# Layer 3's rows normalised in turned form, with one PSUM bank for turns, in a four-layer graph-attention kernel

## The chip, the cores and the metric

The kernel runs on one core of a Trainium2 chip. The metric is the device time of one execution in microseconds, the median of several runs. Engines are named TensorE (PE), VectorE (DVE), ScalarE (ACT), GpSimd (POOL) and SyncE (SP).

## The reference

Eight graphs (B = 8) share one adjacency of 2048 nodes, with 64 features each. Four attention layers follow one another, and each reads a layer-normed, rectified copy of x and adds its result to x:

```
def _layernorm(x, axis=-1, eps=1e-05):
    m = jnp.mean(x, axis=axis, keepdims=True)
    v = jnp.var(x, axis=axis, keepdims=True)
    return (x - m) / jnp.sqrt(v + eps)
...
h = jnp.maximum(_layernorm(x, axis=-1), 0.0)
x = x + _L2_gnn_ref(h, adj, L2_gnn_weight, L2_gnn_query, L2_gnn_key_p)
h = jnp.maximum(_layernorm(x, axis=-1), 0.0)
x = x + _L3_gnn_ref(h, adj, L3_gnn_W, L3_gnn_a)
```

The case is about the place where the third layer's attention (layer 2 in the code, scores q·k with a leaky slope of 0.01) ends and the rows of the last layer (layer 3) are made from its result: x + attention, normalised over the 64 features, rectified, and multiplied by `L3_gnn_W`.

## The kernel before

The nodes are sorted by their number of neighbours into 16 tiles of 128 rows (`NT` = 16). A row holds all eight graphs, 8 x 64 = 512 values (`E`). `X[:, t, :]` is tile t of the running x. Attention runs in five units, `u` = 0 to 4. Unit 3 is layer 2's attention and unit 4 is layer 3's. A tile t has `SLOTS[t]` neighbour rows; for t = 0 to 15 these are 2, 3, 4, 4, 5, 5, 6, 7, 13, 8, 7, 6, 5, 5, 4, 3.

Each engine runs its own instructions in the order in which they are written, in a loop over steps m, and waits at semaphores. There is no scheduler. In step m of unit 3:

- DVE ends the softmax of tile m-1 (`divide`), multiplies the gathered rows of tile m with its query and reduces them (`multiply`, `reduce`, L1908 and L1912), subtracts the maximum (`lower`), sums the squares of tile m-3 (`variance`, L1823), ends the norm of tile m-4 (`end_norm`, L1829), adds the attention of tile m-2 to X (L2041), and takes the mean of that tile (`row_mean`, L1815 and L1816).
- POOL centres tile m-3 (L790), scales its share of tile m-1's rows (`weigh`, L806), gathers the rows of tile m+2 (L779) and scatters the finished rows of tile m-6 into layer 3's table (L828).
- ACT scales its share of tile m-1's rows (`weigh`, L1092: 8, 16, 24, 32 or 48 instructions), copies tile m-2's aggregate for PE (L1200), squares tile m-3 (L1053), takes the two roots of tile m-4 (L1057, L1060), copies the turned tile m-5 (`take_turned`, L990), copies the two projected halves of tile m-6 to `nstage` (`halves`, L1003), copies the turned own rows of tile m+2 (L990), and takes the exponentials of tile m (L1074).
- PE makes the queries of tile m+1 (L1550), turns the normed tile m-5 (L1370), projects tile m-6 (`half`, L1388), turns tile m+2's own rows (L1370), multiplies tile m-2's aggregate with the weights (L1570, into bank 6, which L2041 reads), and adds up the scaled rows of tile m-1 (`add_up`, L1466).

Turns ("transposes") pass through PSUM bank 2 or 3 in alternation, so that a turn waits for the copy of the turn before the last. The two halves of a projection go to banks 7 and 1.

The same norm in turned form exists already in layer 0: ACT copies a turned tile (L990), PE centres it with the matrix `centring` (L1405), ACT squares it (L1025), PE averages the squares with the matrix `averaging` (L1411), ACT takes the logarithm and the exponential over 512 columns (L1031, L1033), and DVE multiplies (L1761).

Unit 4 gathers from the table that unit 3's scatters write: POOL waits for all 16 scatters (`pair_scattered`) before its first gather.

Of the kernel before, what the change touches and what calls it, by code (L numbers as in the profile page):

```python
# [7 lines left out]
ALU = mybir.AluOpType  # L8
# [148 lines left out]
def program(nc, x, adj, L0_W, L0_a, L0_gamma, L0_beta, L1_Wh, L1_bh, L1_Wo, L1_bo, L1_gamma, L1_beta,  # L157
# [14 lines left out]
    with ctx:  # L172
# [129 lines left out]

        def turn_bank(k):
            return bank(2 if k < NT else 2 + k % 2)

# [261 lines left out]
        def _(sp):  # L567
# [39 lines left out]
            def near():  # L607
# [108 lines left out]
        def _(pool):  # L716
# [49 lines left out]
            def near():  # L766
# [77 lines left out]
                for u in range(NU):  # L844
# [94 lines left out]
        def _(act):  # L939
# [45 lines left out]
            def take_turned(to):  # L985

                k = turns[0]
                turns[0] += 1
                act.wait_ge(turned, k + 1)
                act.activation(to, turn_bank(k), ACT.Copy).then_inc(turn_freed, 1)  # L990

            def halves(l, t, parts):

                if 0 <= t < NT:
                    for q in parts:
                        m = 2 * (NT * (l // 3) + t) + q
                        act.wait_ge(half_projected, m + 1)
                        if m >= NPS:
                            act.wait_ge(half_stored[m % NPS], 16 * (m // NPS))
                        if l == 3 and t >= 2:  # L1000
                            act.wait_ge(pair_scattered[t % 2], 16 * (t // 2))
                        b = bank(4 + q) if l == 0 else bank(7 - 6 * q)
                        act.activation(nstage[:, m % NPS, :], b[:, 0:4 * RW], ACT.Copy).then_inc(half_staged, 1)  # L1003
# [41 lines left out]
            def near():  # L1045
# [147 lines left out]
                for m in range(-2, NT + 10):  # L1193
                    weigh(3, m - 1, 0)
                    t = m - 2
                    if 0 <= t < NT:
# [3 lines left out]
                        act.activation(aT[:, t % 2, :], bank(0), ACT.Copy).then_inc(aggT_made, 1)  # L1200
                    norm(3, m - 3)
                    s = m - 5
                    if 0 <= s < NT:
                        if s >= 2:
                            act.wait_ge(half_projected, 2 * (NT + s - 1))
# [116 lines left out]
        def _(pe):  # L1322
# [50 lines left out]
            def turn_in_ring(rows):  # L1373
# [3 lines left out]
                if k >= 1:  # L1377
                    pe.wait_ge(turn_freed, k if k <= NT else k - 1)
                return turn(turn_bank(k), rows).then_inc(turned, 1)

            def half(l, t, q, hT_):

                m = 2 * (NT * (l // 3) + t) + q
                b = bank(4 + q) if l == 0 else bank(7 - 6 * q)
                if t >= 1:
                    pe.wait_ge(half_staged, m - 1)
# [45 lines left out]
            def near():  # L1432
# [110 lines left out]
                for m in range(-2, NT + 10):  # L1543
                    t = m + 1
                    if 0 <= t < NT:
# [6 lines left out]
                        mm.then_inc(q_made, 1)  # L1552
                    if 0 <= m - 5 < NT:
                        pe.wait_ge(h_made, 2 * NT + m - 5 + 1)
                        turn_in_ring(norm_rows(3, m - 5))
                    if 0 <= m - 6 < NT:
                        pe.wait_ge(turn_freed, TURN_OF["next", m - 6] + 1)
# [124 lines left out]
        def _(dve):  # L1682
# [124 lines left out]
            def near():  # L1807
# [199 lines left out]
                for u in (2, 3):  # L2007
                    for m in range(NT + 10):
# [275 lines left out]
```

## Time and profile before

| | |
|---|---|
| median of 3 runs | 1465.96 us (1465.49 to 1466.02) |
| the profiled execution | 1465.91 us |
| its span | 1464.2 us, so 1.7 us lie around it |
| DVE busy | 1195.2 us (82%) |
| POOL busy | 960.1 us (66%) |
| PE busy | 956.3 us (65%) |
| ACT busy | 855.2 us (58%) |
| unit 3, from its first gather to its last scatter | 1101.7 to 1313.5 us |

The span is the time from the first to the last instruction of the profiled execution. A row of a timeline has the start in us from the beginning of the span, the duration in us, engine, line, operation, output and input with shapes, how many instructions are merged in it, and in brackets the idle time before it with what ended it. PE records one product of 128 columns as two instructions, so that a group of four turns shows as x4 and a group of four products as x8.

### The profile page before, as it was taken

The numbers are of one execution on the slowest core, as the hardware profiler recorded it, in microseconds if no ns is written. First come the engines' busy times: TensorE is split into PE (matmuls) and PEld (weight loads), VectorE is DVE, ScalarE is ACT, GpSimd is POOL, SyncE is SP. The second block draws the span as 40 slices with busy tenths as digits, with TensorE's granted clock in tenths as the row PEclk, the third lists the DMA queues.
The fourth block names the chain that finished last, engine by engine and source line by source line (L and its number), as shares of the span: only waits on it lengthen the run. The fifth ranks groups of instructions, "written<-read, shape, count | busy, mean of one in ns | idle before, by whom it ended". The sixth has DMA issues, their size and how long they took to land. (4 is left out here: it accounts for less than half of the span.)

```text
span 1464.2 us, 16972 instructions
## 1 busy us (share of the span) xinstructions
PE 956.3 (65%) x4663; PEld 672.8 (46%) x4663; DVE 1195.2 (82%) x1552; ACT 855.2 (58%) x2899; POOL 960.1 (66%) x983
## 2 busy tenths in 40 slices
PE   3665447542898886498899966566616755756591
PEld 1433113212687775387788832222205655652240
DVE  5994689985999999999999159999976998947571
ACT  5864336664575465356787726777983548654330
POOL 4214776626887866398787468887666787647770
PEclk9887777866899998799999987877856777887796
DMA  9838987514222431012111054533226564438875
GB/s 286 272 102 299 323 243 239 167 58 141 60 83 84 117 92 37 29 35 75 51 51 37 30 166 134 146 115 110 84 97 189 156 185 115 132 119 248 240 236 139
DMA packets 108294, 202.19 MB, mean 138 GB/s; under 512 B 48320, under 2 KB 56800, under 8 KB 106144
## 3 DMA queue, kind: packets, MB, share of 16 engines
q0 software_dynamic: 38384, 128.36, 28.6%
q1 hardware_dynamic: 68840, 72.46, 15.6%
q8 instruction: 40, 0.66, 0.2%
q14 instruction: 62, 0.51, 0.1%
q10 hardware_dynamic: 968, 0.21, 0.1%
HBM read 149.97 MB, written 55.21 MB: 140 GB/s over the span
## 5 line engine op out<-in xcount | busy, mean ns | idle before, releaser
L1092 ACT ACTIVATE big<-big 128x64 f32<-128x64 f32 x1496 | 370.8, 339 | 172.1 <-DVE big L1869 161.0
L806 POOL TENSOR_TENSOR big<-big 128x512 f32<-128x512 f32 x373 | 376.5, 1040 | 123.0 <-DVE big L1869 108.1
L1912 DVE TENSOR_REDUCE big<-big 128x32 f32<-128x2048 f32 (+4 forms) x126 | 297.7, 2362 | 4.3
L1447 PE MATMUL PS<-big,ident 128*128 128x512 f32 x348 | 188.8, 704 | 117.2 <-ACT big L1092 70.5
L1466 PE MATMUL PS<-ident,big 128*128 128x128 f32 x1740 | 232.5, 294 | 42.2 <-POOL big L806 35.1
L1466 PEld LDWEIGHTS PS<-ident,big 128*128 128x128 f32 x1740 | 218.4, 154 | 52.1 <-issue 24.8
L1904 DVE TENSOR_TENSOR big<-big,PS 128x2048 f32<-128x2048 f32 (+4 forms) x84 | 198.5, 2363 | 17.3 <-PE PS L1478 14.5
L1447 PEld LDWEIGHTS PS<-big,ident 128*128 128x128 f32 x348 | 76.3, 226 | 228.0 <-issue 203.8
L779 POOL DMA_INDIRECT big<-tab,SI x142 | 138.0, 972 | 48.6 <-issue 45.0
L779 POOL DMA_INDIRECT big<-h_rows,SI x142 | 137.9, 971 | 38.4 <-issue 29.3
L1463 PE MATMUL PS<-big,ident 128*128 128x512 f32 x174 | 105.9, 769 | 55.3 <-POOL big L806 51.8
L1492 PEld LDWEIGHTS PS<-WoB,big 128*128 128x128 f32 x1024 | 126.0, 194 | 31.1 <-issue 31.1
L1908 DVE TENSOR_TENSOR big<-big,PS 128x2048 f32<-128x2048 f32 (+4 forms) x42 | 99.3, 2363 | 46.3 <-DMA big<-h_table,SI 35.0
L1074 ACT ACTIVATE big<-big 128x32 f32<-128x32 f32 (+11 forms) x80 | 20.6, 258 | 189.7 <-DVE big L1849 189.7
L1492 PE MATMUL PS<-WoB,big 128*128 128x128 f32 x1024 | 126.1, 277 | 0.0
L1370 PE MATMUL PS<-ident,big 128*128 128x128 f32 x320 | 54.5, 305 | 95.9 <-DMA big<-own 66.4
L1463 PEld LDWEIGHTS PS<-big,ident 128*128 128x128 f32 x174 | 41.4, 248 | 120.7 <-POOL big L806 72.4
L1370 PEld LDWEIGHTS PS<-ident,big 128*128 128x128 f32 x320 | 42.7, 159 | 104.4 <-DMA big<-own 69.9
L779 POOL DMA_INDIRECT big<-h_table,SI x71 | 69.3, 976 | 22.1 <-issue 18.6
L1478 PE MATMUL PS<-MB,big 128*128 128x256 f32 x256 | 65.1, 401 | 25.8 <-DVE big L1904 24.4
L790 POOL TENSOR_TENSOR big<-big,stats 128x512 f32<-128x512 f32 x48 | 49.8, 1038 | 48.9 <-DVE stats L1816 48.1
L1896 DVE TENSOR_TENSOR big<-big,PS 128x2048 f32<-128x2048 f32 (+6 forms) x32 | 77.5, 2421 | 1.1
(182 smaller groups left out, 1682.3 us busy)
## 6 DMA issues: line engine op xcount, KB each, us to landing
big<-in_adj SPq DMA_DIRECT2D x16, 1024.0 KB, 6.4
own<-big SPq DMA_DIRECT2D x48, 256.0 KB, 2.0
big<-own SPq DMA_DIRECT2D x48, 256.0 KB, 3.4
big<-xs SPq DMA_DIRECT2D x8, 1024.0 KB, 8.7
tab<-big SPq DMA_DIRECT2D x32, 132.0 KB, 2.8
own<-big SPq DMA_DIRECT2D x32, 132.0 KB, 1.9
big<-own SPq DMA_DIRECT2D x16, 264.0 KB, 4.0
big<-in_x SPq DMA_DIRECT2D x16, 256.0 KB, 6.8
```

Of the source, the lines that this page charges most:

```text
L779: pool.indirect_dma_start(out=rowbuf[t % NRB][:, k * w:(k + 1) * w], out_offset=None, in_=tables[u], in_offset=bass.IndirectOffsetOnAxis(a ...
L806: ins = pool.tensor_tensor(bd(wbuf[:, i % NWB, j, :]), bd(rows[:, k + j, :]), over_d(S[:, h, k + j, :], B), ALU.mult)
L1092: ins = act.activation(to, row, ACT.Copy, scale=S[:, h, k + j, b:b + 1])
L1370: mm = pe.transpose(to[:, q * P:(q + 1) * P], rows[:, q * P:(q + 1) * P], ident[:, :])
L1447: mm = pe.matmul(to.rearrange("p (b d) -> p b d", b=B), ident[:, :], rows[:, k, :].rearrange("p (b c) -> p b c", b=B)[:, :, 0:D], start=(k ...
L1463: mm = pe.matmul(to, ident[:, :], wbuf[:, i % NWB, k, :], start=False, stop=last)
L1466: mm = pe.matmul(to[:, q * P:(q + 1) * P], wbuf[:, i % NWB, k, q * P:(q + 1) * P], ident[:, :], start=(first and q == 0), stop=(last and q ...
L1492: mm = pe.matmul(bank(1)[:, q * P:(q + 1) * P], z[:, j % 2, q * P:(q + 1) * P], blocks(WoB[:, h, :, :]), start=(h == 0 and q == 0 and z is ...
L1896: tell(dve.tensor_tensor(v, v, kept_in_bank(n).unsqueeze(3).to_broadcast([P, n, B, D]), ALU.mult), dve_weighed, NT * (u // 4) + t + 1)
L1904: return dve.tensor_tensor(pr.rearrange("p k (q c) -> p k q c", q=4), rows.rearrange("p k (q c) -> p k q c", q=4), q_half(h // 2, h).unsqu ...
L1908: return dve.tensor_tensor(pr, rows, mine.unsqueeze(1).to_broadcast([P, n, E]), ALU.mult)
L1912: run(dve.tensor_reduce(scores(u, t)[:, h, k:k + n, :].rearrange("p k b -> p (k b)"), bd(prod[:, 0:n * E]), AX.X, ALU.add))
```

## The change

Layer 3's norm takes the turned form of layer 0. Away go POOL's centring (L790), ACT's square and roots over 8 columns (L1053, L1057, L1060) and DVE's mean, variance and row-wise end (L1815, L1816, L1823, L1829) for unit 3. In their place X itself is turned. PE gets two products over 512 columns for each tile, ACT a square, a logarithm and an exponential over 512 columns, and DVE one multiply (h3T). All turns go through bank 2 alone, banks 3 and 7 hold the centred tiles, and bank 1 holds the average and then both halves, one after the other. The projection, its staging, its store and its scatter come one step later (m-7 in place of m-6). A line "..." marks what is left out.

```diff
-    for what, t in (("next", m - 5), ("own", m + 2)):
+    for what, t in (("next", m - 3), ("own", m + 2)):
...
-        def turn_bank(k):
-            return bank(2 if k < NT else 2 + k % 2)
+        turn_bank = bank(2)
+        x3T, sq3T, r3T, h3T = work[:, 6:8, :], sqn, hring, work[:, 4:6, :]
+        def c3_bank(t):
+            return bank(3 + 4 * (t % 2))
...  SyncE, GpSimd
-                                store_halves(3, m - 6)
+                                store_halves(3, m - 7)
-                            if u == 3:
-                                centre(3, m - 3)
-                                put_rows(4, m - 6)
+                                put_rows(4, m - 7)
...  ScalarE, halves and step m of unit 3
-                        b = bank(4 + q) if l == 0 else bank(7 - 6 * q)
+                        b = bank(4 + q) if l == 0 else bank(1)
-                    norm(3, m - 3)
+                    s = m - 3
+                        take_turned(x3T[:, s % 2, :])
+                    s = m - 4
+                        act.wait_ge(xc_made, NT + s + 1)
+                        act.activation(sq3T[:, s % 2, :], c3_bank(s), ACT.Square).then_inc(xc_squared, 1)
                     s = m - 5
-                        take_turned(hT3[:, s % 2, :])
-                    halves(3, m - 6, (0, 1))
+                        act.wait_ge(xvar_made, NT + s + 1)
+                        act.activation(r3T[:, s % 4, :], bank(1), ACT.Ln, bias=epsc[:, 0:1]).then_inc(xvar_logged, 1)
+                        act.activation(r3T[:, s % 4, :], r3T[:, s % 4, :], ACT.Exp, scale=-0.5).then_inc(xvar_rooted, 1)
+                    halves(3, m - 7, (0, 1))
...  TensorE, turn_in_ring, half, and step m of unit 3
-                    pe.wait_ge(turn_freed, k if k <= NT else k - 1)
+                    pe.wait_ge(turn_freed, k)
-                if t >= 1:
+                if l == 3:
+                    pe.wait_ge(half_staged, m)
+                elif t >= 1:
                     pe.wait_ge(half_staged, m - 1)
-                        turn_in_ring(norm_rows(3, m - 5))
-                            half(3, m - 6, q, hT3[:, (m - 6) % 2, :])
+                    t = m - 3
+                        pe.wait_ge(sum_used, NT + t + 1)
+                        turn_in_ring(X[:, t, :])
+                    t = m - 5
+                        pe.wait_ge(xc_squared, NT + t + 1)
+                            pe.wait_ge(half_staged, 2 * (NT + t - 2))
+                        pe.matmul(bank(1), averaging[:, :], sq3T[:, t % 2, :], start=True, stop=True).then_inc(xvar_made, 1)
+                    t = m - 4
+                        pe.matmul(c3_bank(t), centring[:, :], x3T[:, t % 2, :], start=True, stop=True).then_inc(xc_made, 1)
+                    t = m - 7
+                        pe.wait_ge(xvar_logged, NT + min(t + 2, NT - 1) + 1)
+                        pe.wait_ge(h0_made, NT + t + 1)
+                            half(3, t, q, h3T[:, t % 2, :])
                     t = m + 2
                         turn_in_ring(rows_of(3, t)[:, 0, :])
...  VectorE, step m of unit 3
-                            variance(3, m - 3)
-                            end_norm(3, m - 4)
                                 tell(dve.tensor_tensor(X[:, t, :], bank(6), X[:, t, :], ALU.add), sum_used, NT + t + 1)
-                            row_mean(3, t)
+                            t = m - 5
+                                dve.wait_ge(xvar_rooted, NT + t + 1)
+                                tell(dve.scalar_tensor_tensor(h3T[:, t % 2, :], c3_bank(t), 0.0, r3T[:, t % 4, :],
+                                                              ALU.max, ALU.mult), h0_made, NT + t + 1)
```

PE, step 12 of unit 3, before: queries, turn of the normed rows, both halves (WB3), turn of the own rows, product for X (WB2), add_up of tile 11.

```order
L1550 MATMUL PS<-MB,big 128x128 x4
L1370 MATMUL PS<-ident,big 128x128 x4
L1388 MATMUL PS<-WB3,big 128x132 x4
L1370 MATMUL PS<-ident,big 128x128 x4
L1570 MATMUL PS<-WB2,big 128x128 x4
L1466 MATMUL PS<-ident,big 128x128 x24
```

The same step with the change (L1572 queries, L1390 turns, L1410 halves, L1607 product for X, L1488 add_up).

```order
L1572 MATMUL PS<-MB,big 128x128 x4
L1390 MATMUL PS<-ident,big 128x128 x4
L1584 MATMUL PS<-big,averaging 128x512
L1590 MATMUL PS<-big,centring 128x512
L1410 MATMUL PS<-WB3,big 128x132 x4
L1390 MATMUL PS<-ident,big 128x128 x4
L1607 MATMUL PS<-WB2,big 128x128 x4
L1488 MATMUL PS<-ident,big 128x128 x24
```

The two products over 512 columns are new. The halves stand where they stood, ahead of the product for X, but now wait for the logarithm of the same step.

ACT, step 12, before: weigh of tile 11, copy of the aggregate, square, two roots, copy of a turn, two halves, copy of a turn, exponentials.

```order
L1092 ACTIVATE big<-big 128x64 x24
L1200 ACTIVATE big<-PS 128x512
L1053 ACTIVATE big<-big 128x512
L1057 ACTIVATE sd<-stats,epsc 128x8
L1060 ACTIVATE stats<-sd 128x8
L990 ACTIVATE big<-PS 128x512
L1003 ACTIVATE big<-PS 128x264 x2
L990 ACTIVATE big<-PS 128x512
L1074 ACTIVATE big<-big 128x40
```

The same step with the change.

```order
L1095 ACTIVATE big<-big 128x64 x24
L1203 ACTIVATE big<-PS 128x512
L993 ACTIVATE big<-PS 128x512
L1216 ACTIVATE big<-PS 128x512
L1224 ACTIVATE big<-PS,epsc 128x512
L1226 ACTIVATE big<-big 128x512
L1006 ACTIVATE big<-PS 128x264 x2
L993 ACTIVATE big<-PS 128x512
L1077 ACTIVATE big<-big 128x40
```

Copy of the turned X (L993), square (L1216), logarithm (L1224) and exponential (L1226) now stand between the weighing and the staging of the halves (L1006).

## Rows read from the trace of the kernel before

**Rows 1.** Page, part 1: busy time of each engine
```profile
PE 956.3 (65%) x4663; PEld 672.8 (46%) x4663; DVE 1195.2 (82%) x1552; ACT 855.2 (58%) x2899; POOL 960.1 (66%) x983
```
**Rows 2.** The chain that ended last, where unit 3 meets unit 4
```profile
1312.55 0.96 DMA tab<-big,SI
...
1316.42 4.96 DMA big<-tab,SI
```
**Rows 3.** Timeline of DVE, steps 8 and 12
```profile
1186.27 2.29 DVE L1908 TENSOR_TENSOR big<-big,PS 128x2048 f32<-128x2048 f32 x1
...
1202.54 0.69 DVE L1823 TENSOR_REDUCE stats<-big 128x8 f32<-128x512 f32 x1
...
1249.87 2.82 DVE L1908 TENSOR_TENSOR big<-big,PS 128x2560 f32<-128x2560 f32 x1
...
1256.81 0.69 DVE L1823 TENSOR_REDUCE stats<-big 128x8 f32<-128x512 f32 x1 [0.31 <-ACT big L1053]
...
1258.42 0.69 DVE L2041 TENSOR_TENSOR big<-PS,big 128x512 f32<-128x512 f32 x1 [0.20 <-PE PS L1570]
...
1260.07 0.23 DVE L1863 TENSOR_REDUCE mx<-big 128x8 f32<-128x40 f32 x1
```
**Rows 4.** Timeline of ACT: weighings (idle before them), a copy
```profile
1117.49 2.02 ACT L1092 ACTIVATE big<-big 128x64 f32<-128x64 f32 x8 [0.77 <-DVE big L1869]
...
1169.67 5.84 ACT L1092 ACTIVATE big<-big 128x64 f32<-128x64 f32 x24 [3.61 <-DVE big L1869]
...
1206.89 11.56 ACT L1092 ACTIVATE big<-big 128x64 f32<-128x64 f32 x48 [4.06 <-DVE big L1869]
...
1224.59 7.75 ACT L1092 ACTIVATE big<-big 128x64 f32<-128x64 f32 x32 [3.03 <-PE PS L1466]
...
1249.87 5.84 ACT L1092 ACTIVATE big<-big 128x64 f32<-128x64 f32 x24 [3.19 <-DVE big L1869]
1255.61 0.58 ACT L1200 ACTIVATE big<-PS 128x512 f32<-128x512 f32 x1
...
1261.26 3.93 ACT L1092 ACTIVATE big<-big 128x64 f32<-128x64 f32 x16 [2.46 <-DVE big L1869]
...
1291.52 2.02 ACT L1092 ACTIVATE big<-big 128x64 f32<-128x64 f32 x8 [2.94 <-DVE big L1869]
```
**Rows 5.** Timeline of PE in unit 3
```profile
1162.44 1.16 PE L1570 MATMUL PS<-WB,big 128*128 128x128 f32 x8 [2.75 <-ACT big L1200]
...
1256.24 2.07 PE L1570 MATMUL PS<-WB,big 128*128 128x128 f32 x8 [3.38 <-ACT big L1200]
...
1262.17 0.60 PE L1370 MATMUL PS<-ident,big 128*128 128x128 f32 x4
1262.60 1.07 PE L1388 MATMUL PS<-WB,big 128*128 128x132 f32 x8
```
**Rows 6.** Timeline of ACT, layer 0's turned norm
```profile
116.58 0.61 ACT L990 ACTIVATE big<-PS 128x512 f32<-128x512 f32 x1
117.06 0.62 ACT L1025 ACTIVATE big<-PS 128x512 f32<-128x512 f32 x1
117.80 0.69 ACT L1031 ACTIVATE big<-PS,epsc 128x512 f32<-128x512 f32 x1
...
129.88 0.39 ACT L1003 ACTIVATE big<-PS 128x264 f32<-128x264 f32 x1 [3.54 <-DMA tab<-big]
```
**Rows 7.** Timeline of PE, layer 0's turned norm
```profile
115.88 1.02 PE L1405 MATMUL PS<-big,centring 128*128 128x512 f32 x2
116.74 1.02 PE L1411 MATMUL PS<-big,averaging 128*128 128x512 f32 x2
...
130.41 1.22 PE L1388 MATMUL PS<-WB,big 128*128 128x132 f32 x4 [3.12 <-ACT big L1003]
```
**Rows 8.** Timelines of DVE and ACT after unit 3's last step with rows
```profile
1301.04 0.69 DVE L2041 TENSOR_TENSOR big<-PS,big 128x512 f32<-128x512 f32 x1
...
1311.53 0.67 ACT L1003 ACTIVATE big<-PS 128x264 f32<-128x264 f32 x2 [0.53 <-DMA tab<-big,SI]
```

More of the change, by code:

```diff
@@ L989, in take_turned @@
                 act.wait_ge(turned, k + 1)
-                act.activation(to, turn_bank(k), ACT.Copy).then_inc(turn_freed, 1)
+                act.activation(to, turn_bank, ACT.Copy).then_inc(turn_freed, 1)
             def halves(l, t, parts):
@@ L1200, in near @@
                         act.activation(aT[:, t % 2, :], bank(0), ACT.Copy).then_inc(aggT_made, 1)
-                    norm(3, m - 3)
+                    s = m - 3
+                    if 0 <= s < NT:
+                        if s >= 2:
+                            act.wait_ge(xc_made, NT + s - 1)
+                        take_turned(x3T[:, s % 2, :])
+                    s = m - 4
+                    if 0 <= s < NT:
+                        act.wait_ge(xc_made, NT + s + 1)
+                        if s >= 2:
+                            act.wait_ge(xvar_made, NT + s - 1)
+                        if s < 2:
+                            act.wait_ge(var_made, 2 * NT)
+                        act.activation(sq3T[:, s % 2, :], c3_bank(s), ACT.Square).then_inc(xc_squared, 1)
                     s = m - 5
                     if 0 <= s < NT:
-                        if s >= 2:
-                            act.wait_ge(half_projected, 2 * (NT + s - 1))
-                        take_turned(hT3[:, s % 2, :])
-                    halves(3, m - 6, (0, 1))
+                        act.wait_ge(xvar_made, NT + s + 1)
+                        if s >= 4:
+                            act.wait_ge(h0_made, NT + s - 3)
+                        else:
+                            ring_free(act, 3 * NT + s)
+                        act.activation(r3T[:, s % 4, :], bank(1), ACT.Ln, bias=epsc[:, 0:1]).then_inc(xvar_logged, 1)
+                        act.wait_ge(xvar_logged, NT + s + 1)
+                        act.activation(r3T[:, s % 4, :], r3T[:, s % 4, :], ACT.Exp, scale=-0.5).then_inc(xvar_rooted, 1)
+                    halves(3, m - 7, (0, 1))
                     if 0 <= m + 2 < NT:
@@ L1377, in turn_in_ring @@
                 if k >= 1:
-                    pe.wait_ge(turn_freed, k if k <= NT else k - 1)
-                return turn(turn_bank(k), rows).then_inc(turned, 1)
+                    pe.wait_ge(turn_freed, k)
+                return turn(turn_bank, rows).then_inc(turned, 1)
             def half(l, t, q, hT_):
                 m = 2 * (NT * (l // 3) + t) + q
-                b = bank(4 + q) if l == 0 else bank(7 - 6 * q)
-                if t >= 1:
+                b = bank(4 + q) if l == 0 else bank(1)
+                if l == 3:
+                    pe.wait_ge(half_staged, m)
+                elif t >= 1:
                     pe.wait_ge(half_staged, m - 1)
@@ L1552, in near @@
                         mm.then_inc(q_made, 1)
-                    if 0 <= m - 5 < NT:
-                        pe.wait_ge(h_made, 2 * NT + m - 5 + 1)
-                        turn_in_ring(norm_rows(3, m - 5))
-                    if 0 <= m - 6 < NT:
-                        pe.wait_ge(turn_freed, TURN_OF["next", m - 6] + 1)
+                    t = m - 3
+                    if 0 <= t < NT:
+                        pe.wait_ge(sum_used, NT + t + 1)
+                        turn_in_ring(X[:, t, :])
+                    t = m - 5
+                    if 0 <= t < NT:
+                        pe.wait_ge(xc_squared, NT + t + 1)
+                        if t >= 3:
+                            pe.wait_ge(half_staged, 2 * (NT + t - 2))
+                        pe.matmul(bank(1), averaging[:, :], sq3T[:, t % 2, :], start=True, stop=True).then_inc(xvar_made, 1)
+                    t = m - 4
+                    if 0 <= t < NT:
+                        pe.wait_ge(turn_freed, TURN_OF["next", t] + 1)
+                        if t >= 2:
+                            pe.wait_ge(h0_made, NT + t - 1)
+                        pe.matmul(c3_bank(t), centring[:, :], x3T[:, t % 2, :], start=True, stop=True).then_inc(xc_made, 1)
+                    t = m - 7
+                    if 0 <= t < NT:
+                        pe.wait_ge(xvar_logged, NT + min(t + 2, NT - 1) + 1)
+                        pe.wait_ge(h0_made, NT + t + 1)
                         for q in range(2):
-                            half(3, m - 6, q, hT3[:, (m - 6) % 2, :])
+                            half(3, t, q, h3T[:, t % 2, :])
                     t = m + 2
@@ L2041, in near @@
                                 tell(dve.tensor_tensor(X[:, t, :], bank(6), X[:, t, :], ALU.add), sum_used, NT + t + 1)
-                            row_mean(3, t)
+                            t = m - 5
+                            if 0 <= t < NT:
+                                dve.wait_ge(xvar_rooted, NT + t + 1)
+                                if t >= 2:
+                                    dve.wait_ge(half_projected, 2 * (NT + t - 1))
+                                tell(dve.scalar_tensor_tensor(h3T[:, t % 2, :], c3_bank(t), 0.0, r3T[:, t % 4, :],
+                                                              ALU.max, ALU.mult), h0_made, NT + t + 1)
                 for m in range(NT + 3):
```

## Prediction

> **What bounds the kernel now.** I read the page's busy shares first. VectorE is the busiest engine with 1195.2 us of the span [rows 1], but a share over five units doesn't say what this place is worth. The chain that ended last says where unit 3's end counts: the last scatter into layer 3's table is issued at 1312.55, and the first gather of unit 4 follows it at 1316.42 [rows 2]. Whatever moves the last scatter moves the end of the kernel by as much, since nothing of unit 4 is changed. So the sum is that of one place, the last scatter.
>
> Next I read the timelines of unit 3 step by step. Let D be the time at which the softmax of tile m-1 is ended in step m. ScalarE's weighing begins there, and so does VectorE's multiply of tile m. In step 12, D is 1249.87 on both engines [rows 3, 4]. VectorE needs M for its multiplies and for `lower`: 6.9 us in step 12 (1249.87 to 1256.81, with 0.3 us idle), 16.3 us in step 8 (1186.27 to 1202.54) [rows 3]. ScalarE needs W for its weighing: 2.02 us for tiles with 8 instructions, 3.93 for 16, 5.84 for 24, 7.75 for 32 and 11.56 for 48 [rows 4]. Then it copies the aggregate (1255.61), TensorE makes the product for X (1256.24, 2.07 us), and VectorE adds to X at 1258.42 [rows 3 to 5]. So the leg L from the end of the weighing (1255.71) to the add is 2.7 us, and the add can begin at D plus the greater of M and W + L. Before, W + L is 8.5 in step 12 while VectorE fills its time with the variance and the end of the norm, and idles only 0.2 us. VectorE is the bound, just.
>
> **What the change takes off VectorE.** The variance is one instruction of 0.69. From the add to the next softmax are 1.65 us (1258.42 to 1260.07), of which 0.72 are the add with its gap, so the two means take 0.93 [rows 3]. The end of the norm stays one instruction of the same 512 columns. VectorE loses 0.72 + 0.93 = 1.65 us a step. The work after the add becomes 0.72 (add) + 0.72 (end of the norm) + 1.2 (1260.07 to 1261.26, the softmax) = 2.65 us [rows 3, 4]. GpSimd loses its centring; its work lies beside ScalarE's weighing and VectorE's multiplies, so I count that at nothing (it would be one instruction a step, some 1 us, if GpSimd were the bound).
>
> **What the change puts on the leg.** TensorE takes its instructions in order, and the halves stand ahead of the product for X. They now wait for the logarithm of the same step, which ScalarE reaches only after its weighing. Behind them on TensorE are queued the turn of the own rows, the product for X, for which VectorE waits, and the adding up, for which ScalarE's next copy waits. So the leg becomes, with durations from layer 0's turned norm:
>
> - The aggregate's copy begins 0.1 before the weighing's end (1249.87 + 5.84 = 1255.71). From one copy to the next are 0.48, taken twice (116.58 to 117.06), from the square to the logarithm 0.74 (117.06 to 117.80), and the logarithm takes 0.69: 2.3 us after the weighing [rows 4, 6].
> - Both halves through one bank: 0.14 until TensorE starts (129.88 + 0.39 = 130.27 to 130.41), 0.60 for four pieces, 0.1 back to ScalarE, 0.39 for the staging copy, 0.14, 0.60 [rows 5 to 7]. Sum 2.0.
> - The turn of the own rows 0.43 (1262.17 to 1262.60), the product 1.16, 0.11 to VectorE (1258.31 to 1258.42), less 0.2 of overlap (a guess, since TensorE's ends are modelled) [rows 3, 5]. Sum 1.5.
>
> **The sum over the steps**, at the upper clock, step = max(M, W + 5.8) + 2.65:
>
> - Steps 2 to 6 took 1117.49 to 1169.67, 52.2 us [rows 4]. The halves are not there yet. The leg grows only by the X copy and the wait for its bank. I take 49.0, gain 3.2 (1.65 a step less about one of new wait, since there the product ran mostly at the lower clock).
> - Steps 7 and 8 took 1169.67 to 1206.89, 37.2 [rows 4]. New: 5.84 + 5.8 + 2.25 = 13.9, then 16.3 + 2.7 = 19.0, since M covers the leg. Gain 4.3.
> - Steps 9 to 15 took 1206.89 to 1291.52, 84.6 [rows 4]. Now W + L is over M in each. Step 9: 11.56 + 8.45 = 20.0. Step 10: 0.5 + 7.75 + 8.45 = 16.7. Steps 11 and 12: 14.3 each. Steps 13 to 15: 12.4 each. Together 102.4, loss 17.8.
>
> At step 16 (before at 1291.52) the changed kernel is 10.3 late.
>
> **The tail.** Before, the add of tile 15 began at 1301.04, 9.5 after step 16's start, and the last scatter at 1312.55 ended one microsecond later, 22.0 after it [rows 2, 4, 8]. New, step 16: 2.02 + 5.4 puts the add of tile 14 at 7.4. In step 17 the turn of X follows at 8.2, both large products end 0.43 + 0.86 + 1.02 later (10.5), square and logarithm 1.5, halves 2.0, product and hand-over 1.0: the add of tile 15 at 15.0 [rows 5 to 7]. Then tile 15 has five more steps to go where before it had four shorter ones. Step 18 takes 2.3 + 0.05 + 1.45 + 2.0 + 0.5 = 6.3, step 19 (no turn) 6.0, step 20 (no centring) 4.4, steps 21 and 22 (halves only, 2 x (0.14 + 0.60 + 0.1 + 0.39)) 2.5 each. With 0.8 for the add and 1.3 from the last staging to the end of the scatter (1312.20 to 1313.51) [rows 2, 8]: 15.0 + 0.8 + 6.3 + 6.0 + 4.4 + 5.0 + 1.3 = 38.8. Loss 16.8.
>
> 10.3 + 16.8 = 27 us at the upper clock.
>
> **TensorE's clock.** Of the 14 products for X in unit 3 that had idle time before them, six had up to 2.75 us, and five of those took 1.16; eight had 3.38 or more, and seven of those took 2.07 or 2.08; one of each kind stands in [rows 5]. In the changed kernel TensorE has done its queries, turn and two large products some 4 us after D, and then idles until W + 2.4: 2.3 us where W is 3.93, 4 us where it is 5.84, 10 us in step 9. So of steps 7, 9, 11 and 12 I count three at the lower clock, 3 x 2.6 = 8. Sum 27 + 8 = 35, on 1465.9: 1501. The overlaps that I could not price, mostly in the tail, make me take 1500. The profiled execution (1465.91) stands within 0.1 us of the median.
>
> The Trainium skill (TensorE: Matmul & The Clock Gate, HAM oscillation — how this bites in real kernels) says that a stream of products broken by waits falls back to half rate at each break. The trace agrees after the long breaks and not after the short ones; by the rule alone the third rival below would be the likeliest.
>
> **The rivals.** *1. The chain as worked out, with a mixed clock*: +14 to +51, chance 0.78. *2. The chain is shorter by some microseconds a step*, because hand-overs overlap more than I take: with L = 4 the nine chain-bound steps give back 16 and the tail about 5, which leaves +3 to +14. For it: VectorE idled only 0.2 us in step 12. Against: each leg is a measured row. Chance 0.08. *3. The lower clock throughout*: 9 steps x 2.6 and some 10 in the tail on top of 27, +60, 1526. For it: the new waits of TensorE. Against: two more large products in each step, and the 1.16 after short idle times. Chance 0.08. *4. VectorE stays the bound*, the other side: its 1.65 us come off in 14 steps, 23 us, less the tail's 16.8, so -6, 1460. It decides where W + L is no more than M, which for W = 5.84 and M = 6.9 asks for L of 1.1, where even the old leg was 2.7. Only a TensorE that takes the halves after the product for X would do that, and its order says the reverse. Chance for faster 0.04, and 0.02 for a sum that falls within 0.2%, 2.9 us, about what a measurement of this kernel can tell from no change.
>
> **How the numbers follow.** The likeliest is +35, taken as 1500. The range takes in case 1 with all its clock uncertainty, from 1480 (L one microsecond shorter in nine steps, the tail 4 shorter, and no slow step) to 1517 (slow clock in six or seven steps and half of the tail). That leaves 0.14 below and 0.08 above, a little more than 2 in 10, so case 1's edges are the range's. Faster 0.04, same 0.02, slower 0.94.
>
> **What the new profile would show.** VectorE idle before the X add in steps 9 to 15, released by the product for X, 2 to 7 us each; TensorE idle before the halves, released by ScalarE's logarithm; no idle before the X add in step 8; steps 9 to 15 some 100 us or more; from step 16 to the last scatter 38 to 45 us; unit 4 as long as before. I am wrong if VectorE's idle before the add stays under 1 us, if the steps from 9 on are no longer than before, or if the tail is under 30 us.

## The result, and the profile after

The changed kernel takes 1498.12 us (median of 4 runs, 1493.97 to 1500.06) against 1465.72 us for the kernel before. The ratio is 1.0219, with a 95% interval of 1.0195 to 1.0243. The forecast was 1500, slower. The profiled execution is the fastest of the four, 1493.97 us with a span of 1492.1 us.

The page's busy times answer to [rows 1]:

```profile
PE 982.5 (66%) x4727; PEld 681.1 (46%) x4727; DVE 1161.4 (78%) x1504; ACT 870.5 (58%) x2899; POOL 941.2 (63%) x967
```

VectorE works 34 us less (the prediction's 1.65 us a tile make 26 for 16 tiles), ScalarE 15 and TensorE 26 us more, and the kernel is 28 us longer in this execution. Busy time doesn't tell where that comes from. The timelines of step 12 do (its start was 1249.87 before, and is 1246.27 here). ScalarE, which answers to [rows 4]:

```profile
1246.27 5.84 ACT L1095 ACTIVATE big<-big 128x64 f32<-128x64 f32 x24 [2.57 <-DVE big L1906]
1252.01 0.58 ACT L1203 ACTIVATE big<-PS 128x512 f32<-128x512 f32 x1
1252.49 0.58 ACT L993 ACTIVATE big<-PS 128x512 f32<-128x512 f32 x1
1252.96 0.58 ACT L1216 ACTIVATE big<-PS 128x512 f32<-128x512 f32 x1
1253.44 0.68 ACT L1224 ACTIVATE big<-PS,epsc 128x512 f32<-128x512 f32 x1
1254.15 0.63 ACT L1226 ACTIVATE big<-big 128x512 f32<-128x512 f32 x1
1255.46 0.39 ACT L1006 ACTIVATE big<-PS 128x264 f32<-128x264 f32 x1 [0.68 <-PE PS L1410]
1257.19 0.39 ACT L1006 ACTIVATE big<-PS 128x264 f32<-128x264 f32 x1 [1.33 <-PE PS L1410]
```

TensorE in the same step, which answers to [rows 5]:

```profile
1249.04 1.02 PE L1590 MATMUL PS<-big,centring 128*128 128x512 f32 x2
1254.17 1.25 PE L1410 MATMUL PS<-WB,big 128*128 128x132 f32 x4 [4.12 <-ACT big L1224]
1255.90 1.25 PE L1410 MATMUL PS<-WB,big 128*128 128x132 f32 x4 [0.48 <-ACT big L1006]
1256.94 1.06 PE L1390 MATMUL PS<-ident,big 128*128 128x128 f32 x4
1257.80 1.92 PE L1607 MATMUL PS<-WB,big 128*128 128x128 f32 x8
```

VectorE, which answers to [rows 3]:

```profile
1259.82 0.69 DVE L2076 TENSOR_TENSOR big<-PS,big 128x512 f32<-128x512 f32 x1 [6.88 <-PE PS L1607]
```

The reader is to see one thread through the three. The copied aggregate (L1203) is ready at 1252.59. The product that reads it (L1607) starts only at 1257.80, because both halves and a turn stand ahead of it, and the first half had waited for the logarithm (L1224). VectorE idles 6.88 us before its add. From the end of the weighing (1252.11) to the add are 7.7 us, where it was 2.7 before.

Who waited for whom from step 9 to the last scatter (us in total, times, longest), where L833 is the scatter and L1006 the staging of a half:

```profile
POOL tab L833 <- ACT big L1006: 65.4, 14, 8.2
DVE big L2076 <- PE PS L1607: 54.1, 9, 8.9
```

The last scatter and unit 4's first gather, which answer to [rows 2]:

```profile
1342.49 0.97 POOL L833 DMA_INDIRECT tab<-big,SI  x1 [2.55 <-ACT big L1006]
1346.03 0.99 POOL L784 DMA_INDIRECT big<-tab,SI  x1 [2.57 <-issue]
```

Unit 3 can be cut at the starts of ScalarE's weighing, which marks the start of each step. "Tail" is from the start of step 16 to the end of the last scatter. The whole times of the experiments stand beside a kernel before of 1460.4 us (1458.5 us for the changed kernel on another chip), and the changed kernel's 1498.12 us beside one of 1465.72 us, so the ratio and the stretches are what to compare. A ratio is the recorded one of all runs with its 95% interval, and not the quotient of the two medians.

| us | steps 2 to 6 | steps 7, 8 | steps 9 to 15 | tail | sum |
|---|---|---|---|---|---|
| kernel before | 52.2 | 37.2 | 84.6 | 22.0 | 196.0 |
| changed kernel | 43.9 | 34.1 | 105.4 | 44.8 | 228.2 |
| changed kernel, another chip | 44.1 | 33.7 | 105.7 | 44.9 | 228.4 |
| product first | 43.0 | 32.4 | 88.2 | 40.8 | 204.4 |
| product and exponentials first | 42.1 | 33.5 | 84.4 | 40.7 | 200.7 |
| two banks in the tail | 44.0 | 34.0 | 105.5 | 30.4 | 213.9 |
| more products | 44.3 | 33.6 | 95.2 | 44.9 | 218.0 |
| all three (without the products) | 41.9 | 33.9 | 84.5 | 26.9 | 187.2 |
| before, one bank for turns | 52.2 | 37.2 | 92.5 | 22.9 | 204.8 |
| before, one bank for halves | 53.0 | 36.8 | 103.7 | 30.5 | 224.0 |
| halves sooner | 41.2 | 32.9 | 76.3 | 24.4 | 174.8 |

Unit 3 costs 32.2 us more than before. The profiled execution is longer by 27.9 only, since step 2 began 2.2 us earlier (1115.3 for 1117.5) and unit 4 took 2.1 us less (148.6 for 150.7 from the last scatter to the span's end).

### The profile page after: what moved, and what is told of

Its sections match the earlier page's. It is cut to its first block and busy times, and to the rows that moved or that the text cites. A ratio compares the mean times of both kernels' runs of the same rounds, so it can differ in the third digit from the quotient of the medians.

```text
span 1492.1 us, 17048 instructions
## 1 busy us (share of the span) xinstructions
PE 982.5 (66%) x4727; PEld 681.1 (46%) x4727; DVE 1161.4 (78%) x1504; ACT 870.5 (58%) x2899; POOL 941.2 (63%) x967
## 3 DMA queue, kind: packets, MB, share of 16 engines
q0 software_dynamic: 38384, 128.36, 27.9%
## 5 line engine op out<-in xcount | busy, mean ns | idle before, releaser
L1469 PE MATMUL PS<-big,ident 128*128 128x512 f32 x348 | 185.9, 694 | 117.1 <-ACT big L1095 70.9
L1488 PE MATMUL PS<-ident,big 128*128 128x128 f32 x1740 | 223.8, 287 | 37.9 <-POOL big L811 33.5
L1488 PEld LDWEIGHTS PS<-ident,big 128*128 128x128 f32 x1740 | 210.8, 150 | 47.1 <-POOL big L811 22.2
L1485 PE MATMUL PS<-big,ident 128*128 128x512 f32 x174 | 105.1, 765 | 61.7 <-POOL big L811 56.9
L1390 PE MATMUL PS<-ident,big 128*128 128x128 f32 x320 | 55.8, 310 | 94.9 <-DMA big<-own 64.6
L1485 PEld LDWEIGHTS PS<-big,ident 128*128 128x128 f32 x174 | 41.2, 247 | 125.8 <-POOL big L811 77.8
L1390 PEld LDWEIGHTS PS<-ident,big 128*128 128x128 f32 x320 | 43.8, 162 | 104.5 <-DMA big<-own 67.2
L1410 PE MATMUL PS<-WB,big 128*128 128x132 f32 x256 | 51.4, 344 | 60.9 <-ACT big L1224 46.7
L1500 PE MATMUL PS<-MB,big 128*128 128x256 f32 x256 | 68.6, 417 | 26.8 <-DVE big L1941 25.4
L1410 PEld LDWEIGHTS PS<-WB,big 128*128 128x128 f32 x256 | 42.4, 234 | 87.1 <-ACT big L1224 59.8
```

The source lines that it names most:

```text
L1390: mm = pe.transpose(to[:, q * P:(q + 1) * P], rows[:, q * P:(q + 1) * P], ident[:, :])
L1410: mm = pe.matmul(b[:, i * 2 * RW:(i + 1) * 2 * RW], hT_[:, (2 * q + i) * P:(2 * q + i + 1) * P], blocks(WB[l][:, 0, :, :]), start=True, st ...
L1469: mm = pe.matmul(to.rearrange("p (b d) -> p b d", b=B), ident[:, :], rows[:, k, :].rearrange("p (b c) -> p b c", b=B)[:, :, 0:D], start=(k ...
L1485: mm = pe.matmul(to, ident[:, :], wbuf[:, i % NWB, k, :], start=False, stop=last)
L1488: mm = pe.matmul(to[:, q * P:(q + 1) * P], wbuf[:, i % NWB, k, q * P:(q + 1) * P], ident[:, :], start=(first and q == 0), stop=(last and q ...
```

## Experiments

**The product for X first.** The halves move behind the product in TensorE's order (lines cut).

```diff
+                    t = m - 2
+                        pe.wait_ge(aggT_made, NT * HEADS + t + 1)
+                            mm = pe.matmul(bank(6)[:, q * P:(q + 1) * P], aT[:, t % 2, q * P:(q + 1) * P],
+                                           blocks(WB[2][:, 1, :, :]), start=True, stop=True)
                     t = m - 7
                             half(3, t, q, h3T[:, t % 2, :])
                     t = m + 2
                         turn_in_ring(rows_of(3, t)[:, 0, :])
-                    t = m - 2
-                        pe.wait_ge(aggT_made, NT * HEADS + t + 1)
-                            mm = pe.matmul(bank(6)[:, q * P:(q + 1) * P], aT[:, t % 2, q * P:(q + 1) * P],
-                                           blocks(WB[2][:, 1, :, :]), start=True, stop=True)
```

> The changed kernel, with the product for X ahead of both halves in TensorE's order. Theory 1 (the loss lies in what stands ahead of that product: two halves through one bank, behind the logarithm): the leg from the weighing's end to the X add falls from 8 to some 2 to 3 us, VectorE no longer idles before the X add, but it now waits at the softmax, because ScalarE takes the exponentials of tile m only after the halves (some 5.5 us after the weighing). A step is then W + 6.9 or M + 2.65: steps 9 to 15 take some 91 us where the changed kernel took 105, and with the shorter steps 16 and 17 the whole is 1480 (1475 to 1486). Theory 2 (the loss is the amount of work that ScalarE and TensorE got, wherever it stands): same work, 1495 to 1500. Theory 3 (the single bank for turns): 1495 to 1500 as well, since the turns are as before.

Measured: 1472.35 us, ratio 1.0057 (1.0025 to 1.0089). Steps 9 to 15 took 88.2 us. The same instructions in another order give back 17 us there and 4 in the tail, so the amount of work is not what costs that. Part of the 17 us comes by way of the clock: TensorE's granted clock in these steps is 0.90, where it was 0.82. The whole is 2.7 us under the range that I gave. ScalarE and VectorE in step 11:

```profile
1234.79 0.39 ACT L1006 ACTIVATE big<-PS 128x264 f32<-128x264 f32 x1 [0.19 <-PE PS L1410]
1236.51 0.39 ACT L1006 ACTIVATE big<-PS 128x264 f32<-128x264 f32 x1 [1.34 <-PE PS L1410]
1237.70 0.60 ACT L993 ACTIVATE big<-PS 128x512 f32<-128x512 f32 x1 [0.80 <-PE PS L1390]
1238.20 0.23 ACT L1077 ACTIVATE big<-big 128x48 f32<-128x48 f32 x1
```
```profile
1233.93 0.69 DVE L2076 TENSOR_TENSOR big<-PS,big 128x512 f32<-128x512 f32 x1
1236.61 0.69 DVE L2082 SCALAR_TENSOR_TENSOR big<-PS,big 128x512 f32<-128x512 f32 x1 [1.99 <-PE PS L1410]
1238.53 0.24 DVE L1900 TENSOR_REDUCE mx<-big 128x8 f32<-128x48 f32 x1 [1.23 <-ACT big L1077]
```

In this step the add (L2076) waits for nothing, and in the others from 9 to 15 for 3.1 us at most, where it waited up to 9. Two waits took its place: the end of the norm (L2082) waits for the second half, which frees the h3T buffer, and the softmax (L1900) waits for exponentials that ScalarE takes only after the halves. I had expected the second, not the first.

**Exponentials first as well.**

```diff
+                    exp(3, m)
                     halves(3, m - 7, (0, 1))
...
-                    exp(3, m)
```

> As e1, and ScalarE takes the exponentials of tile m ahead of the staging of the halves. Theory 1: a step is the greater of M + 2.65 and W + 4.4, so steps 9 to 15 take 75 to 80 us, less than the 84.6 of the kernel before; the tail after step 16 keeps some 16 us of its loss. Together 1465 to 1472. Theory 2 (amount of work): 1495 or more. If e1 and e2 come out alike, the softmax's wait was not what came next.

Measured: 1467.95 us, ratio 1.0039 (1.0016 to 1.0062). The whole lies in the range given, but steps 9 to 15 took 84.4 us, not 75 to 80, which is no less than in the kernel before (84.6). The softmax's wait went, the wait for the halves stayed, and ScalarE is idle only some 0.5 us before each of the weighings of steps 11 to 13 (the last row is cut by the view's window, which is why it has 13 instructions):

```profile
1240.42 0.69 DVE L2082 SCALAR_TENSOR_TENSOR big<-PS,big 128x512 f32<-128x512 f32 x1 [1.63 <-PE PS L1410]
```
```profile
1241.88 3.21 ACT L1095 ACTIVATE big<-big 128x64 f32<-128x64 f32 x13 [0.47 <-DVE big L1906]
```

My rule "M + 2.65 or W + 4.4" left the buffer's wait out.

**Two banks in the tail.** Halves of tiles 10 to 15 go to banks 4 and 5, which no query needs by then, and don't wait for the logarithm.

```diff
-                        b = bank(4 + q) if l == 0 else bank(1)
+                        b = bank(4 + q) if l == 0 or t >= 10 else bank(1)
...
-                if l == 3:
-                    pe.wait_ge(half_staged, m)
+                if l == 3 and t < 11:
+                    pe.wait_ge(half_staged, m if t < 10 else 2 * (NT + 10))
...
-                        pe.wait_ge(xvar_logged, NT + min(t + 2, NT - 1) + 1)
+                        if t < 10:
+                            pe.wait_ge(xvar_logged, NT + t + 3)
```

> The changed kernel, where the halves of tiles 10 to 15 (steps 17 to 22) go to banks 4 and 5, which hold no queries by then, and do not wait for the logarithm. Theory 1 (one bank for the average and both halves costs the tail its round trips): from step 16 to the last scatter 28 to 31 us in place of 44.8, the steps before unchanged, 1483 (1480 to 1487). Rival (the tail is long because tile 15 has one step more to go and longer instructions): 40 us or more, 1493 to 1498.

Measured: 1480.81 us, ratio 1.0142 (1.0109 to 1.0174). The tail fell from 44.8 to 30.4 us and nothing else moved (105.5 against 105.4). This is 14 of the 23 us that the tail had lost. The edit takes away two waits at once, for the bank and for the logarithm, and with them goes the lower clock that the tail had (granted clock 0.76 before this edit). These were not run apart. The tail's row, in the form of the window rows of the next experiment:

```profile
1301.20:1331.57 30.37, 22.39 (x117) 16.01 (x115) 4.84 (x7) 17.44 (x41) 8.85 (x9) 0.94 0.31 113
```

Its last two scatters are 1.95 us apart, where the changed kernel's last two are 3.5 apart (1338.97 and 1342.49):

```profile
1328.65 0.97 POOL L833 DMA_INDIRECT tab<-big,SI  x1 [0.89 <-ACT big L1006]
1330.60 0.97 POOL L833 DMA_INDIRECT tab<-big,SI  x1 [0.98 <-ACT big L1006]
```

**More products.** 40 products of 512 columns (the expectation says 41, but the edit's list adds up to 40) fill TensorE's idle time before the halves. They write bank 6, which the product for X writes over, so the output is unchanged.

```diff
+                    for i in range({7: 4, 8: 4, 9: 13, 10: 3, 11: 3, 12: 4, 13: 2, 14: 3, 15: 3, 16: 1}.get(m, 0)):
+                        pe.matmul(bank(6), centring[:, :], x3T[:, (m - 4) % 2, :], start=True, stop=True)
```

> The changed kernel with 1 to 13 products more a step in steps 7 to 16 (41 in all, 512 columns each, into bank 6, which the product for X writes over), which fill TensorE's idle time before the halves. If TensorE's lower clock after those idle times makes the leg long, both halves fall from 1.25 to 0.72 us each, the turn and the product get shorter, and 1.5 to 2.6 us go in each of steps 9, 10, 11, 12, 14 and 15: 1486 (1483 to 1490). If the clock is no part of it, the time stays at 1495 to 1500, or rises where a filling product ends late.

Measured: 1479.06 us, ratio 1.0144 (1.0103 to 1.0184), less than the changed kernel although it computes more, and 3.9 us under the range that I gave. TensorE in step 12 (1235.69 to 1249.14):

```profile
1239.32 3.60 PE L1592 MATMUL PS<-big,centring 128*128 128x512 f32 x8
1243.60 0.72 PE L1410 MATMUL PS<-WB,big 128*128 128x132 f32 x4 [0.69 <-ACT big L1224]
1244.80 0.72 PE L1410 MATMUL PS<-WB,big 128*128 128x132 f32 x4 [0.48 <-ACT big L1006]
1245.36 0.60 PE L1390 MATMUL PS<-ident,big 128*128 128x128 f32 x4
1245.79 1.06 PE L1609 MATMUL PS<-WB,big 128*128 128x128 f32 x8
```

Each half takes 0.72 for 1.25, the turn 0.60 for 1.06, the product 1.06 for 1.92. Steps 9 to 15 by stretch (us, busy of PE, PEld, DVE, ACT, POOL, then granted clock, DMA share, GB/s), first the changed kernel, then this one:

```profile
1193.23:1298.63 105.40, 70.50 (x414) 59.91 (x413) 63.36 (x81) 70.63 (x237) 51.69 (x53) 0.82 0.32 99
```
```profile
1187.60:1282.77 95.17, 86.38 (x483) 60.72 (x482) 63.34 (x81) 70.63 (x237) 52.15 (x53) 0.99 0.36 110
```

ScalarE's busy time is the same to 0.01 us, VectorE's to 0.02. The granted clock rises from 0.82 to 0.99, which is nearly all of the time at the upper level of 2.4 GHz, and the stretch is 10.2 us shorter. So the changed kernel would lose 10.6 us in these steps in place of 20.8 if its TensorE stayed at the upper clock. That isn't to say that the change brought the lower clock. The kernel before had a granted clock of 0.81 in its steps 9 to 15, about the same:

```profile
1206.89:1291.52 84.63, 53.63 (x384) 51.59 (x383) 77.31 (x102) 63.24 (x237) 58.09 (x58) 0.81 0.38 114
```

There, of TensorE's slow work only the product for X stood between ScalarE's weighing and VectorE's add. In the changed kernel two halves and a turn stand there as well. What a steady upper clock would give the kernel before was not run. The Trainium skill (TensorE: Matmul & The Clock Gate, HAM oscillation — how this bites in real kernels) says that products broken by long waits keep falling back to the lower clock. This pair of runs agrees, with 10.2 us as its price here. The prediction took the short breaks, after which the product for X still took 1.16 us, as speaking against the section. They don't: its example has waits longer than the work between them.

**All three edits** (product first, exponentials first, tail banks).

> Product for X first, exponentials first, and tiles 10 to 15's halves in banks 4 and 5 (e1, e2 and e3 together). If the two costs lie in different stretches, they add: e2's 84.4 us for steps 9 to 15 and e3's 30 us from step 16 to the last scatter (less what e2's earlier product gives steps 16 and 17, so 25 to 29), which makes 7 us less than the kernel before. If they share a cause, the sum is worse: as long as the kernel before, or longer.

Measured: 1452.08 us, ratio 0.9936 (0.9914 to 0.9958). The stretches are those of the parts. Steps 9 to 15 took 84.5 us (84.4 in the second experiment). The tail took 26.9: from 44.8, the first experiment had taken off 4.0 and the third 14.4, which makes 26.4. The savings add, and the whole is 8.3 us less than the kernel before, for 7.

**The kernel before with one bank for turns.**

```diff
-            return bank(2 if k < NT else 2 + k % 2)
+            return bank(2)
...
-                    pe.wait_ge(turn_freed, k if k <= NT else k - 1)
+                    pe.wait_ge(turn_freed, k)
```

> The kernel before with all turns through bank 2, nothing else. Theory 3 (the single bank for turns is a cost of its own): the turn of the own rows now waits for ScalarE's copy of the normed tile, some 2.0 us after the weighing's end, with the product for X behind it, so the leg grows from 2.7 to about 4.2: some 8 us more over steps 9 to 15, nothing in the tail, +6 to +10. Rival (the bank is no cost, the changed kernel's loss is all in the halves and the logarithm): within 2 us of the kernel before.

Measured: 1472.11 us, ratio 1.0073 (1.0046 to 1.01), that is +11.8 us on the medians, where I had 6 to 10. Steps 9 to 15 took 7.9 us more and the tail 0.9. The other 3 us lie outside the table's stretches. TensorE in step 12:

```profile
1248.97 1.08 PE L1370 MATMUL PS<-ident,big 128*128 128x128 f32 x4 [5.11 <-ACT big L990]
1249.85 1.91 PE L1570 MATMUL PS<-WB,big 128*128 128x128 f32 x8
```

The turn of the own rows waits for ScalarE's copy, with the product for X behind it.

**The kernel before with one bank for both halves.**

```diff
-                        b = bank(4 + q) if l == 0 else bank(7 - 6 * q)
+                        b = bank(4 + q) if l == 0 else bank(1)
...
+                if l == 3:
+                    pe.wait_ge(half_staged, m)
```

> The kernel before with both halves through bank 1, nothing else. Theory 1: the second half waits for the staging of the first, which ScalarE reaches some 1.9 us after its weighing; the product for X stands behind it, so the leg grows to 4.7 us or more: +12 to +16 in all, of which 2 to 4 in the tail. Rival (the halves' order alone is harmless without the logarithm's wait): within 2 us of the kernel before.

Measured: 1488.21 us, ratio 1.0186 (1.0151 to 1.0222), +27.9 us on the medians. Steps 9 to 15 took 19.1 us more and the tail 8.5. This one edit of a bank, with no new work, costs nearly what the whole change costs (ratio 1.0186 beside 1.0219). TensorE in step 11:

```profile
1244.91 0.62 PE L1390 MATMUL PS<-WB,big 128*128 128x132 f32 x4
1251.09 1.25 PE L1390 MATMUL PS<-WB,big 128*128 128x132 f32 x4 [5.56 <-ACT big L1003]
```

I had 12 to 16. The missing part is the lower clock after the idle time: the second half takes 1.25 where the first takes 0.62, and the granted clock fell from 0.81 to 0.75 in steps 9 to 15 and from 0.92 to 0.77 in the tail. That this is all of it is read from these rows; no run held the clock up here.

**Halves sooner.** On top of all three edits, the halves return to m-6, and the second comes behind the turn of the own rows, on TensorE and ScalarE alike.

```diff
-                    halves(3, m - 7, (0, 1))
+                    exp(3, m)
+                    halves(3, m - 6, (0,))
...
                         take_turned(hTo[:, m % 2, :])
+                    halves(3, m - 6, (1,))
```

> As e5, and the halves come at m-6 as in the kernel before, the first ahead of the turn of the own rows and the second behind it, on TensorE and on ScalarE. In e2 VectorE's last multiply still waited 1.6 us a step for the halves of two tiles before, and ScalarE was idle only 0.5 us between steps, so it was the bound with W + 5.5. Both go: steps 9 to 15 take 75 to 79 us (ScalarE bound, W + 4.4, or VectorE, M + 2.65), the tail 25 to 28, and the whole is 14 to 20 us less than the kernel before. If that wait was only filling time that ScalarE needs anyway, steps 9 to 15 stay over 82 us.

Measured: 1439.3 us, ratio 0.9861 (0.9832 to 0.9891): faster than the kernel before by 1.4%, and than the changed kernel by 3.5 to 4% (by its two ratios, 1.0219 and 1.0257). Steps 9 to 15 took 76.3 us, as given, and the tail 24.4, a little less than the 25 to 28 given. ScalarE's end of step 11 and the next weighing:

```profile
1233.42 0.22 ACT L1077 ACTIVATE big<-big 128x40 f32<-128x40 f32 x1
1233.66 0.39 ACT L1006 ACTIVATE big<-PS 128x264 f32<-128x264 f32 x1
1234.16 0.60 ACT L993 ACTIVATE big<-PS 128x512 f32<-128x512 f32 x1
1234.86 0.39 ACT L1006 ACTIVATE big<-PS 128x264 f32<-128x264 f32 x1
1235.15 1.05 ACT L1095 ACTIVATE big<-big 128x64 f32<-128x64 f32 x4
```

No row carries an idle time, and none of the weighings of steps 11 to 15 does: ScalarE is the bound there, and the wait for a bank lies under the copy that came between. The earlier step for the halves and their new order were not run apart.

**The changed kernel again.**

> The changed kernel once more, for a comparison on another chip, since the kernel before took 1465.7 us beside the first timing and 1460.4 beside the experiments. If the 13 us by which whole executions differ come from the part ahead of unit 3 (its step 2 began at 1104 to 1117 us in the traces so far), steps 9 to 15 take 105 to 106 us and the tail 43 to 46 again, and the ratio is 1.019 to 1.025. If the stretches of unit 3 themselves vary, the comparisons by stretch are worth less than they look.

Measured: 1496.82 us against 1458.5 for the kernel before, ratio 1.0257 (1.0223 to 1.0291), a little over the 1.019 to 1.025 that I gave. By stretches (44.1, 33.7, 105.7, 44.9) it repeats the first trace within 0.5 us. Across all traces the start of step 2 ranged from 1109.7 to 1118.1 (the expectation's 1104 was the start of step 1), so whole times differ by what lies ahead of unit 3 more than unit 3 does.

## Why the prediction was right, point by point

**VectorE stops being the bound: right.** It loses three instructions a tile, and its idle time before the add is 2.7 to 9.0 us in steps 9 to 15 (released by L1607 each time). In step 8 the add doesn't wait, as M covers the leg.

**The leg: right in cause, and a little shorter at both ends.** I had 5.8 us at the upper clock and 8.4 at the lower. Weighing's end to add took 5.4 in step 13 (1265.93 to 1271.35, halves of 0.72), 7.7 in steps 9 and 12 (halves of 1.25). VectorE's idle time of 2.7 to 9.0 us was forecast as 2 to 7. The first experiment shows the cause: with the product ahead of the halves the leg is 1.8 to 2.8 us in steps 9 to 15, and the wait is gone in step 11. What the logarithm's wait and the one bank for both halves each put on the leg of the changed kernel was not run apart. TensorE's strict order is what makes it; the Trainium skill (TensorE: Matmul & The Clock Gate, Step-by-step: what each phase is for) says that only weight loads are pulled ahead and products stay in program order, and the trace agrees: the product was held 5.2 us with its input ready (1252.59 to 1257.80).

**Steps 2 to 6: mis-sized.** I took a gain of 3.2, it was 8.3. I let the product run mostly at the lower clock there. It did so in step 3, but the adds of steps 5 and 6 had no wait before them, and the gain was 1.66 us a step. VectorE's busy time (the third of the busy times in a window row) fell by more, 10.3 us or 2.06 a step, and its idle time grew by 2.0. Steps 2 to 6 before and after:

```profile
1117.49:1169.67 52.18, 35.48 (x212) 34.17 (x212) 49.51 (x67) 28.66 (x101) 41.27 (x42) 0.77 0.52 157
```
```profile
1115.26:1159.12 43.86, 31.55 (x201) 27.57 (x202) 39.23 (x52) 29.50 (x99) 34.52 (x36) 0.84 0.56 167
```

So the term "VectorE loses 1.65 us a step" was itself about 0.4 us too small; the last section has the instruction that it left out.

**Steps 7 and 8:** gain 3.1 for 4.3. Of the gain that I gave, 0.4 is a slip: step 7 has 2.25 us after the leg, where the rule's own 2.65 belongs. Its halves ran at the lower clock (1.25 us each), which I had put into the clock's term.

**Steps 9 to 15:** loss 20.8, for 17.8 at the upper clock plus most of the 8 that I had put on the clock for steps 7, 9, 11 and 12. The clock's price in these steps is 10.2 by the fourth experiment, so without it they lose 10.6, where I had 17.8. Three terms were too dear: the leg at the upper clock by 0.4 us, the work after the add by 0.5 (2.18 from 1259.82 to 1262.00, for 2.65), and in steps 14 and 15 I had counted a turn of own rows that these steps don't have. The clock's own term was too small by 2 to 5 us, depending on how much of the 8 fell to step 7. I had named steps 7, 9, 11 and 12. Both halves took 1.25 us in steps 7, 8, 9, 12 and 15, and the second one in step 11. Step 10 I had left out without a reason, although my own formula gave it 6 us of idle time. It had 3.24, its halves took no more than 0.72, and its product for X 1.91.

**The tail: mis-sized.** Loss 22.8 for 16.8. The add of tile 15 came 16.2 us after step 16's start (1298.63 to 1314.83), for 15.0. The rest, 4.8 us, I put down to the lower clock in steps 19 to 22, for which my sum has nothing in the tail: the large products of step 19 took 1.80 and 1.91 for 1.02, the average of step 20 2.04, and the last six halves 1.22 to 1.25 each. The granted clock of the stretch is 0.76:

```profile
1298.63:1343.46 44.83, 30.55 (x118) 19.41 (x116) 4.84 (x7) 18.55 (x41) 8.85 (x9) 0.76 0.22 79
```

The errors offset: 5.1 us too little gain at the start against a tail that was 6.0 too short. The sum for unit 3 is 32.2 for 35. That 1500 lies 2 us from the median is luck in good part, by these errors and because whole executions of the changed kernel spread over 6 us. The direction and the leg are not.

**What I had left out.** The end of the norm waits for the halves of two tiles before (`half_projected`), because h3T has two buffers and the halves come at m-7. In the changed kernel this wait is under the longer one. It shows when that goes.

**One bank for turns** costs 7.9 us in steps 9 to 15 by itself, one bank for halves 19.1. In the changed kernel both waits end on the same ScalarE sequence after the weighing, so they don't add: it lost 20.8 there. That they end on the same sequence is read from the order of the instructions. How much is the turn's and how much the halves' within the changed kernel was not tried apart.

## What to carry to other kernels

Before moving work off the busiest engine, write down what stands ahead of the instruction that this engine waits for, on each in-order engine, and what each of those waits for. Two waits that point to an engine in the middle of a long run of its own put that run on the path, even if they are only the price of a saved PSUM bank. The idle time that they make can also put the work behind them at the lower clock. Here the idea was good and the order was not: the same norm with the product first, the exponentials first, and the halves put where banks are free turns 2.2% slower into 1.4% faster. When such a wait is mended, read the trace for the wait that lay beneath it.

## What the runs showed of the hardware

40 products that nobody reads made the kernel faster, by 10.2 us in the stretch of steps 9 to 15, with the busy times of ScalarE and VectorE the same. On whole executions the gain is 18 us by the medians (1496.82 to 1479.06, on two chips whose kernels before took 1458.5 and 1460.35), or 11 us by the ratios 1.0219 and 1.0144, or 17 by 1.0257 and 1.0144. TensorE's granted clock there went from 0.82 to 0.99. What the two medians show beyond 10.2 us lies ahead of step 2, which began at 1118.07 in the one trace and at 1109.69 in the other, 8.4 us apart with the same instructions ahead of it. I can't say what made that, and it is no gain of the edit as far as is shown.

The softmax's last small multiply got shorter with no edit of its own. In unit 3 of the kernel before, steps 2 to 16, it took 0.61 to 1.36 us in the 12 steps in which GpSimd's centring ran beside it, and 0.18 to 0.22 in the three in which it didn't. Two of 48 columns, without and with the centring:

```profile
1169.43 0.21 DVE L1869 TENSOR_TENSOR big<-big,mx 128x48 f32<-128x48 f32 x1
1249.18 0.65 DVE L1869 TENSOR_TENSOR big<-big,mx 128x48 f32<-128x48 f32 x1
```

VectorE and GpSimd in the kernel before, step 12:

```profile
1260.57 0.65 DVE L1869 TENSOR_TENSOR big<-big,mx 128x40 f32<-128x40 f32 x1
```
```profile
1260.13 1.03 POOL L790 TENSOR_TENSOR big<-big,stats 128x512 f32<-128x512 f32 x1 [0.67 <-DVE stats L1816]
```

In the changed kernel the same multiply has GpSimd idle beside it and takes 0.20:

```profile
1261.77 0.20 DVE L1906 TENSOR_TENSOR big<-big,mx 128x40 f32<-128x40 f32 x1
```

In the kernel before it ended 0.06 us after the centring did (1261.22 and 1261.16), and the one of 1.36 us did too (1157.94 and 1157.88). In the changed kernel, which has no centring on GpSimd, all 15 took 0.18 to 0.27. So VectorE's multiply waits for GpSimd's centring by all these rows, though no run moved the centring alone. It is the 0.45 us a step by which the work after the add was shorter than I had.
